# Two six-layer stacks on one core: the layer loops written out, and semaphore increments placed in front of some visits to small products on TensorE

## The chip, the cores and the metric

The kernel runs on one core of a Trainium2 chip. The metric is the device time of one launch in microseconds (us). Five engines work side by side, each through its own instruction stream: TensorE (PE; its weight loads are listed as PEld), VectorE (DVE), ScalarE (ACT), GpSimd (POOL) and SyncE (SP), which starts the DMA transfers. A "q" behind an engine's name (PEldq, SPq) marks what its sequencer does by itself: waits on semaphores, register work, branches and the start of transfers.

## The reference, cut to what matters

```python
x = L0_attn_a_X                                    # 8 x 256 x 128, f32
x = x + retention(layernorm(x))
x = x + ffn_stack(layernorm(x))                    # run 0
x = x + rwkv(layernorm(x))                         # mix and scan
x = x + ffn_stack(layernorm(x))                    # run 1

def ffn_stack(x):                                  # 6 layers, 2,048 rows of 128
    for i in range(6):
        x = attn_layer(shift_tokens(x), ...) + x   # 16 heads of 64, windows of 32 rows, each looking at 64 keys
        x = ffn_layer(shift_tokens(x), ...) + x    # layer norm, 128 -> 341 gated -> 128
    return x
```

The windowed attention is why there are small products: for each window of 32 queries and each head, a 32x64 block of scores, and then a 64x32 block of the weighed values. Everything is float32.

## The kernel before

The kernel has four parts: a retention layer, a stack (run 0), the mix-and-scan part, and a second stack (run 1). Both stacks come from `ffn_stack` and are the same code. The change touches the stacks alone.

**Tiling.** A stack works on tiles of 128 rows. There are 16 tiles in a layer and 96 (`TILES`) in a stack, 192 in all. Four tiles make a group (`GROUPS`), the unit of the feed-forward part. Work is cut into slots. In slot N each engine does pieces of several tiles, each with its lag: TensorE projects tile N-4, transposes tiles N-5 and N-6, computes the scores of tile N-6, weighs the values of tile N-9, projects out tile N-10, and does a quarter of the feed-forward part of an older group. The four kinds of slot (T = N mod 4, T0 to T3 in this text) are written out by hand in `slot`, one for each engine, and the order in them is fixed.

**TensorE's pieces.** `project` (L608) is a 128x512 product; `turn` (L617) four transpositions of 128x128; `project_out` (L668) eight accumulating 128x128 products; `center`, `variance`, `up` and `down` (L675, L682, L691, L701) the feed-forward part. `scores` (L632) is 64 products of 64x32 by 64x64, issued in two calls, and `weigh` (L655) is 64 products of 64x64 by 64x32, also in two calls. The text calls the 64 products of one tile a *visit*: there is one scores visit and one weigh visit for each tile. Each float32 product is two weight loads and two MATMULs in the stream of the chip, so a visit has 256 rows; a transposition has one of each.

**What sets the order.** Semaphores alone. [...] `apart` (L467) increments the semaphore `passed`, on which nobody waits; in front of a wait whose value is in a register it keeps waits in separate rows. For a slot whose number is a plain integer `apart` does nothing.

**The loops.** `slots` (L483 to L493) runs slots 0 to 15 written out, slots 16 to 79 as a hardware loop (`Fori`, L491) of two passes over 32 slots, and the last 32 written out. The four compute engines have this loop, and SyncE has one over layers 1 to 4 (L582). In the loops the slot's number is a register, so each wait value is worked out by register rows.

```python
            run_slots(0, 0, 0, 0, 16)
            with eng.Fori(0, 2) as pair:
                run_slots(32 * pair + 16, 8 * pair + 4, 2 * pair + 1, 1, 32)
            run_slots(16 * (DEPTH - 1), 4 * (DEPTH - 1), DEPTH - 1, 1, 16 + 16)
```

Of the kernel before, what the change touches and what calls it, by code (L numbers as in the profile page):

```python
# [20 lines left out]
DEPTH, HEADS, HD, WINDOW = 6, 16, 64, 32  # L21
# [318 lines left out]
RSQRT_SHIFT = 16  # L340
TABLE = "natural_log_exp_and_others"
GELU_TABLE = "gelu_and_others"


Group = namedtuple("Group", ("number", "layer", "row", "pair", "half"))
# [2 lines left out]
def ffn_stack(nc, shared, w):  # L348

    xo, ident, rot, mask = shared["x"], shared["ident"], shared["rot"], shared["mask"]  # L350
    with ExitStack() as ctx:
# [124 lines left out]
        def slots(eng, body):  # L476

            def run_slots(tile, group, layer, odd, slots_run):  # L480
                for n in range(slots_run):
                    def of(lag, k=n // 4):
                        return Group(group + (k - lag), layer + (k - lag) // 4, (k - lag) % 4, (k - lag) % 2,  # L483
                                     (odd + (k - lag) // 4) % 2)

                    def at(lag, n=n):
                        return tile + (n - lag), (n - lag) % 4, of(0, (n - lag) // 4)
                    body(tile + n, n % 4, group + n // 4, at, of)

            run_slots(0, 0, 0, 0, 16)  # L490
            with eng.Fori(0, 2) as pair:  # L491
                run_slots(32 * pair + 16, 8 * pair + 4, 2 * pair + 1, 1, 32)
            run_slots(16 * (DEPTH - 1), 4 * (DEPTH - 1), DEPTH - 1, 1, 16 + 16)  # L493

        block = ctx.enter_context(nc.Block())

# [1 line left out]
        def _(sp):  # L498
# [80 lines left out]
            load_mlp(0)  # L579
            sp.wait_ge(consts_set, N_CONSTS * (run + 1))  # L580
            layer_loads(0, True, False)
            with sp.Fori(1, DEPTH - 1) as layer:  # L582
                layer_loads(layer, False, False)
            layer_loads(DEPTH - 1, False, True)
            sp.wait_ge(wo_in, 16 * (layer0 + DEPTH))
# [13 lines left out]
        def _(pe):  # L599
# [11 lines left out]
            def turn(t, T, g, c):  # L611
                if not live(t):
                    return
                wait(pe, "united_" + c, t)
                bank = work[(BANK["t_" + c][T] + g.row) % 4]
                for n in range(4):
                    last = pe.transpose(bank[:, P * n:P * (n + 1)], roped[:, CHUNKS.index(c), T % 2, P * n:P * (n + 1)],  # L617
                                        ident[:, :])
                last.then_inc(done["turned_" + c], 1)

            def scores(t, T, g, part):
                if not live(t):
# [99 lines left out]
            def slot(N, T, G, at, of):  # L722
                if T == 0:
# [5 lines left out]
                    project(*at(4), "q0")  # L729
                    wait(pe, "kept_k0", N - 6)  # L730
                    up(of(4), "lin", 1)
                    wait(pe, "ot_set", N - 10)
                    weigh(*at(9), 0)
                    weigh(*at(9), 1)
# [5 lines left out]
                    project(*at(7), "v1")  # L740
                    wait_group(pe, "hid1", G - 4)
                    project(*at(4), "k1")
                    wait(pe, "masked0", N - 7)
                    wait(pe, "masked1", N - 7)
                    scores(*at(6), 0)
# [11 lines left out]
                elif T == 1:  # L757
                    wait(pe, "mid_set", N - 11)
                    project(*at(4), "k0")
                    wait(pe, "ot_set", N - 10)  # L760
                    weigh(*at(9), 0)
                    weigh(*at(9), 1)
# [16 lines left out]
                    project(*at(4), "k1")  # L779
                    wait(pe, "kept_k1", N - 6)  # L780
                    project(*at(4), "q1")
                    wait(pe, "masked0", N - 7)
                    wait(pe, "masked1", N - 7)
                    scores(*at(6), 0)
# [5 lines left out]
                elif T == 2:  # L790
# [5 lines left out]
                    center(of(3))  # L796
                    wait(pe, "kept_k0", N - 6)
                    down(of(4))
                    wait(pe, "ot_set", N - 10)
                    weigh(*at(9), 0)  # L800
                    weigh(*at(9), 1)
# [7 lines left out]
                    project(*at(4), "q1")  # L809
                    wait(pe, "kept_q0", N - 6)  # L810
                    project(*at(4), "k1")
                    wait(pe, "masked0", N - 7)
                    wait(pe, "masked1", N - 7)
                    scores(*at(6), 0)
# [17 lines left out]
                elif T == 3:  # L832
                    wait(pe, "v_out0", N - 6)
                    project(*at(4), "k0")
                    wait(pe, "ot_set", N - 10)
                    weigh(*at(9), 0)
                    weigh(*at(9), 1)
                    wait(pe, "kept_q0", N - 6)
                    project(*at(5), "v0")
                    wait(pe, "kept_k1", N - 6)  # L840
                    turn(*at(6), "q1")
                    wait(pe, "squared_q0", N - 4)
                    project(*at(7), "v1")
                    wait(pe, "squared_k0", N - 4)
                    project(*at(4), "k1")
                    wait(pe, "masked0", N - 7)
                    wait(pe, "masked1", N - 7)
                    scores(*at(6), 0)
                    scores(*at(6), 1)
                    wait(pe, "v_out0", N - 5)  # L850
                    up(of(3), "gate", 2)
                    wait(pe, "kept_q1", N - 6)
                    project(*at(4), "q1")
                    wait(pe, "v_out1", N - 7)
                    up(of(3), "gate", 0)
                    wait(pe, "squared_k1", N - 4)
                    project_out(*at(10))
                    wait_group(pe, "gelu2", G - 3)
                    turn(*at(5), "q0")
                    wait(pe, "squared_q1", N - 4)  # L860
                    up(of(3), "gate", 1)
                    wait_group(pe, "gelu0", G - 3)
                    turn(*at(5), "k0")
# [1745 lines left out]
```

## Time and profile before

| what | value |
|---|---|
| median of 3 runs | 3645.67 us (3636.82 to 3646.73) |
| the profiled execution: its own time | 3648.2 us |
| its span | 3646.4 us |
| mean granted TensorE clock | 0.967 of full speed |
| TensorE busy (MATMUL) | 3373.7 us, 93% |
| VectorE busy | 3341.6 us, 92% |
| GpSimd busy | 2706.3 us, 74% |
| ScalarE busy | 2049.2 us, 56% |

The span runs from the first to the last instruction of the profiled execution; its own time is 1.8 us more, for what lies around it. Shares of busy time are averages over the retention part, the two stacks and the part between them, which has its own limits. A MATMUL's end is modelled, so a small gap between two of them can be hidden in the busy time. A gap that is put down to "issue" is time in which the engine waited for nothing that the profile shows. The profile also lists each DMA queue. Queue q8 carries kind "instruction".

### The profile page before, as it was taken

How to read it: one execution, taken by the hardware profiler on the slowest of the kernel's cores; microseconds unless marked ns; L12 is line 12 of the kernel's file. 1: busy time of each engine (PE TensorE's matmuls, PEld its weight loads, DVE VectorE, ACT ScalarE, POOL GpSimd, SP SyncE). 2: the span in 40 equal slices, each digit the busy share in tenths (PEclk: the TensorE clock that was granted, in tenths of full speed). 3: DMA queues.
4: the chain of work that ended last, by engine and by line, in shares of the span. 5: the costliest groups of instructions: out<-in, count | busy, mean ns of one | idle time of the engine just before them, and what ended most of it. 6: DMA issues, size and time to landing. Idle time of an engine off the chain costs nothing. (4 is left out here: it accounts for less than half of the span.)

```text
span 3646.4 us, 153624 instructions
## 1 busy us (share of the span) xinstructions
PE 3373.7 (93%) x60144; PEld 2186.3 (60%) x60144; DVE 3341.6 (92%) x11899; ACT 2049.2 (56%) x3659; POOL 2706.3 (74%) x2440
## 2 busy tenths in 40 slices
PE   6799999999999999987699689999999999999997
PEld 4366666666666666652466446666666666666664
DVE  6899999999999999965799799999999999999995
ACT  2456666656665666644422155666666566666663
POOL 1788888888888888843144288888888888888882
PEclk9899999999999999998799699999999999999999
DMA  1233333333333333320000123333333333333332
GB/s 44 61 89 83 74 89 75 90 78 79 91 76 76 87 80 71 72 66 16 1 1 0 36 49 88 79 89 79 74 93 75 77 84 82 73 89 77 72 72 65
DMA packets 151851, 250.83 MB, mean 69 GB/s; under 512 B 42688, under 2 KB 73408, under 8 KB 150976
## 3 DMA queue, kind: packets, MB, share of 16 engines
q1 hardware_dynamic: 151104, 240.75, 27.7%
q8 instruction: 484, 7.93, 1.0%
q14 instruction: 263, 2.15, 0.2%
HBM read 38.21 MB, written 1.05 MB: 11 GB/s over the span
## 5 line engine op out<-in xcount | busy, mean ns | idle before, releaser
L608 PE MATMUL stack_work<-stack_w_qkv,stack_xst 128*128 128x512 f32 x2304 | 1173.6, 615 | 26.9 <-ACT stack_sq L881 16.7
L1337 POOL TENSOR_TENSOR stack_roped<-stack_rot_c,stack_rot_s 128x512 f32<-128x512 f32 x768 | 980.6, 1289 | 260.1 <-DVE stack_rot_s L1082 135.0
L1347 POOL TENSOR_TENSOR stack_roped<-stack_roped,stack_rnorm 128x512 f32<-128x512 f32 x768 | 791.5, 1044 | 162.4 <-DVE stack_rnorm L1114 162.4
L881 ACT ACTIVATE stack_sq<-stack_work 128x512 f32<-128x512 f32 x768 | 457.3, 595 | 735.0 <-DVE stack_rot_s L1082 727.5
L1080 DVE TENSOR_TENSOR stack_rot_c<-stack_work,rot_tables 128x512 f32<-128x512 f32 x768 | 517.0, 673 | 56.5 <-PE stack_work L608 52.0
L608 PEld LDWEIGHTS stack_work<-stack_w_qkv,stack_xst 128*128 128x128 f32 x2304 | 387.3, 193 | 300.5 <-issue 226.5
L1082 DVE TENSOR_TENSOR stack_rot_s<-stack_work,rot_tables 128x512 f32<-128x512 f32 x768 | 519.3, 676 | 1.1 <-issue 1.1
L1091 DVE TENSOR_REDUCE stack_ssq<-stack_sq 128x8 f32<-128x512 f32 x768 | 512.4, 672 | 3.3
L1125 DVE CUSTOM_DVE_ANT_0 stack_s_m<-stack_bank_s,band 128x64 f32<-128x64 f32 x3072 | 469.5, 215 | 30.1 <-PE stack_bank_s L632 26.4
L617 PEld LDWEIGHTS stack_work<-ident,stack_roped 128*128 128x128 f32 x3072 | 354.1, 141 | 167.4 <-issue 143.5
L617 PE MATMUL stack_work<-ident,stack_roped 128*128 128x128 f32 x3072 | 436.4, 277 | 19.3 <-ACT stack_sq L881 11.6
L1363 POOL TENSOR_TENSOR stack_s_m<-stack_s_m,stack_inv 128x512 f32<-128x512 f32 x384 | 412.6, 1074 | 37.8 <-DVE stack_inv L1143 37.8
L1355 POOL TENSOR_TENSOR stack_s_m<-stack_s_m,stack_smax 128x512 f32<-128x512 f32 x384 | 401.6, 1046 | 37.3 <-DVE stack_smax L1125 35.2
L655 PEld LDWEIGHTS stack_bank_o<-stack_p_pairs,stack_v_even 64*64 64x64 f32 x12288 | 330.0, 134 | 155.8 <-issue 155.6
L668 PEld LDWEIGHTS stack_work<-stack_o_t,stack_w_o 128*128 128x128 f32 x3072 | 364.5, 192 | 77.4 <-issue 63.8
L632 PEld LDWEIGHTS stack_bank_s<-stack_k_t,stack_q_t 64*32 64x32 f32 x24576 | 276.6, 105 | 206.2 <-issue 200.1
L655 PE MATMUL stack_bank_o<-stack_p_pairs,stack_v_nat 64*64 64x32 f32 x12288 | 378.2, 219 | 16.6 <-issue 16.5
L655 PE MATMUL stack_bank_o<-stack_p_pairs,stack_v_even 64*64 64x32 f32 x12288 | 378.8, 220 | 12.4 <-issue 8.8
L668 PE MATMUL stack_work<-stack_o_t,stack_w_o 128*128 128x128 f32 x3072 | 368.2, 275 | 5.2 <-issue 4.7
L632 PE MATMUL stack_bank_s<-stack_k_t,stack_q_t 64*32 64x64 f32 x24576 | 318.5, 225 | 48.0 <-issue 47.6
L655 PEld LDWEIGHTS stack_bank_o<-stack_p_pairs,stack_v_nat 64*64 64x64 f32 x12288 | 333.4, 135 | 20.2 <-issue 20.1
L907 ACT COPY stack_q_t<-stack_work 128x512 f32<-128x512 f32 x384 | 226.8, 591 | 169.0 <-PE stack_work L617 168.2
(255 smaller groups left out, 5093.2 us busy)
## 6 DMA issues: line engine op xcount, KB each, us to landing
stack_v_even<-stack_v_nat SPq DMA_DIRECT2D x768, 128.0 KB, 2.4
stack_p_pairs<-stack_p_turned SPq DMA_DIRECT2D x1536, 64.0 KB
stack_w_qkv<-table_ffn_qkv SPq DMA_DIRECT2D x192, 96.0 KB
stack_w_o<-table_ffn_wo SPq DMA_DIRECT2D x12, 512.0 KB, 3.9
stack_w<-table_ffn_w SPq DMA_DIRECT2D x12, 384.0 KB, 3.2
stack_w<-table_ffn_w SPq DMA_DIRECT2D x12, 192.0 KB, 3.0
x_outer<-L_attn_a_X SPq DMA_DIRECT2D x4, 256.0 KB, 8.1
ret_xpos<-table_xpos SPq DMA_DIRECT2D x1, 1024.0 KB, 7.5
```

The lines of the kernel that those rows point to most:

```text
L608: pe.matmul(work[(BANK["p_" + c][T] + g.row) % 4][:, :], xst[:, g.row, P * T:P * (T + 1)], w_qkv[:, g.half, col:col + 512], start=True, st ...
L617: last = pe.transpose(bank[:, P * n:P * (n + 1)], roped[:, CHUNKS.index(c), T % 2, P * n:P * (n + 1)], ident[:, :])
L632: last = pe.matmul(bank_s[j][WINDOW * n:WINDOW * (n + 1), 64 * hp:64 * hp + 64], q_t[rows, T % 2, hp, WINDOW * n:WINDOW * (n + 1)], k_t[ro ...
L655: last = pe.matmul(bank_o[HD * odd:HD * (odd + 1), two, at:at + WINDOW], values[:, 2 * m + j, :], p_pairs[rows, T % 2, odd_window, j, 2 * ...
L668: last = pe.matmul(bank[:, 0:P], w_o[:, g.half, n, :], o_t[:, T % 2, n, :], start=n == 0, stop=n == PAIRS - 1)
L881: act.activation(sq[:, i % 2, :], work[(BANK["p_" + c][T] + g.row) % 4][:, :], ACT.Square).then_inc(done["squared_" + c], 1)
L1080: dve.tensor_tensor(rot_c[:, i % 2, :].rearrange("p (h d) -> p h d", h=8), src.rearrange("p (h d) -> p h d", h=8), cosine, ALU.mult)
L1082: dve.tensor_tensor(rot_s[:, i % 2, :].rearrange("p (h f d) -> p h f d", h=8, f=2), src.rearrange("p (h f d) -> p h f d", h=8, f=2)[:, :, ...
L1091: dve.tensor_reduce(ssq[:, T % 2, i, :], sq[:, i % 2, :].rearrange("p (h d) -> p h d", h=8), AX.X, ALU.add).then_inc(done["summed_" + c], 1)
L1125: last = dve.tensor_tensor_reduce(s_m[:, T % 2, j, hp, :], bank_s[j][:, 64 * hp:64 * hp + 64], mask[:, first:first + 2 * WINDOW], 1.0, LOW ...
L1337: pool.tensor_tensor(roped[:, i, T % 2, :], rot_c[:, i % 2, :], rot_s[:, i % 2, :], ALU.add).then_inc(done["roped_" + c], 1)
L1347: pool.tensor_tensor(r, r, rnorm[:, T % 2, i, :].unsqueeze(2).broadcast_to([P, 8, HD]), ALU.mult).then_inc(done["united_" + c], 1)
```

## The change

It does three things.

1. `slots` no longer has a loop: all 112 slots of a stack are written out on the four compute engines, and SyncE's loop over layers 1 to 4 is a Python loop. All slot numbers are now integers, so the register rows, the branches and the increments of `apart` in the stacks are gone.
2. A table `SETTLE` gives, for each kind of visit, each run and each tile, a number of increments.
3. `settle` issues that many increments of `passed` on TensorE, each a semaphore row of its own, ahead of the waits that stand in front of the visit: before `wait(pe, "ot_set", N - 10)` for weigh, before `wait(pe, "masked0", N - 7)` for scores. Nothing waits on `passed`.

The order of all products, transfers and other work on every engine is as before.

```diff
+SETTLE = {
+    "scores": (
+        (0, 0, 0, 0, 0, 50, 0, 27, 0, 0, 0, 0, 0, 0, 0, 0, 0, 0, 0, 0, 0, 0, 0, 0,
...
+        (23, 59, 0, 126, 0, 0, 0, 0, 0, 0, 0, 0, 0, 0, 0, 0, 0, 0, 0, 0, 0, 0, 0, 0,
...
+    "weigh": (
+        (68, 0, 0, 0, 0, 0, 0, 0, 0, 37, 0, 27, 0, 43, 0, 27, 0, 43, 0, 27, 0, 43, 0, 27,
...
+         0, 43, 0, 27, 0, 43, 0, 27, 0, 43, 0, 27, 0, 43, 0, 27, 0, 43, 0, 36, 0, 0, 51, 0),
+        (0, 0, 0, 30, 0, 62, 0, 27, 0, 43, 0, 27, 0, 43, 0, 27, 0, 43, 0, 27, 0, 43, 0, 27,
...
+         0, 43, 0, 27, 0, 43, 0, 27, 0, 43, 0, 27, 0, 43, 0, 27, 0, 43, 0, 36, 0, 0, 51, 0),
...
-            run_slots(0, 0, 0, 0, 16)
-            with eng.Fori(0, 2) as pair:
-                run_slots(32 * pair + 16, 8 * pair + 4, 2 * pair + 1, 1, 32)
-            run_slots(16 * (DEPTH - 1), 4 * (DEPTH - 1), DEPTH - 1, 1, 16 + 16)
+            run_slots(0, 0, 0, 0, TILES + 16)
...
-            with sp.Fori(1, DEPTH - 1) as layer:
+            for layer in range(1, DEPTH - 1):
                 layer_loads(layer, False, False)
...
+            def settle(t, T, g, kind):
+                if live(t):
+                    for _ in range(SETTLE[kind][run][t]):
+                        pe.sem_inc(passed, 1)
...
                     up(of(4), "lin", 1)
+                    settle(*at(9), "weigh")
                     wait(pe, "ot_set", N - 10)
                     weigh(*at(9), 0)
                     weigh(*at(9), 1)
...
                     project(*at(4), "k1")
+                    settle(*at(6), "scores")
                     wait(pe, "masked0", N - 7)
                     wait(pe, "masked1", N - 7)
                     scores(*at(6), 0)
```

The two calls are added in the same way in all four kinds of slot. The table holds 3,526 increments. In its steady part, 41 times in a row over both runs, four tiles get 27 in front of one weigh visit (in a T0 slot, behind `up`) and 43 in front of another (in a T2 slot, behind `down`): 2,870 increments. The other 656 stand in front of 17 visits near the ends of the stacks, with 23 to 126 each.

## Rows read from the trace of the kernel before

**Rows 1.** The page: span, busy time, and 40 slices of PE and its clock.

```profile
span 3646.4 us, 153624 instructions
PE 3373.7 (93%) x60144; PEld 2186.3 (60%) x60144; DVE 3341.6 (92%) x11899; ACT 2049.2 (56%) x3659; POOL 2706.3 (74%) x2440
...
PE   6799999999999999987699689999999999999997
...
PEclk9899999999999999998799699999999999999999
```

**Rows 2.** Busy time in one stretch of the first stack: us, engines, PEclk, DMA.

```profile
600.00:1000.00 400.00, 386.83 (x7773) 253.09 (x7771) 382.03 (x1464) 247.43 (x445) 334.17 (x306) 0.99 0.34 81
```

**Rows 3.** PE's waits in that stretch: us in total, times, longest.

```profile
PE stack_bank_s L632 <- issue: 7.2, 6, 1.6
PE stack_work L608 <- DMA stack_w_qkv<-table_ffn_qkv: 3.0, 1, 3.0
PE stack_bank_o L655 <- issue: 1.9, 2, 1.4
```

**Rows 4.** The same view over the whole span.

```profile
PE stack_bank_s L632 <- issue: 47.6, 45, 2.0
PE stack_bank_o L655 <- issue: 25.2, 29, 1.9
```

**Rows 5.** PE in time order: a scores visit, then the end of a weigh visit.

```profile
996.58 1.52 PE L632 MATMUL stack_bank_s<-stack_k_t,stack_q_t 64*32 64x64 f32 x122
999.70 0.31 PE L632 MATMUL stack_bank_s<-stack_k_t,stack_q_t 64*32 64x64 f32 x6 [1.60 <-issue]
...
3321.16 0.32 PE L655 MATMUL stack_bank_o<-stack_p_pairs,stack_v_even 64*64 64x32 f32 x8
...
3324.25 0.26 PE L655 MATMUL stack_bank_o<-stack_p_pairs,stack_v_even 64*64 64x32 f32 x5 [1.26 <-issue]
```

**Rows 6.** DMA queues: over the span, then in 3321.5 to 3322.0 us.

```profile
q8 instruction: 484, 7.93, 1.0%
...
q8 instruction: 1, 0.02, 12.9%
```

**Rows 7.** The semaphore row in front of a weigh visit, at four visits.

```profile
L644 PEldq EVENT_SEMAPHORE  x1: 51/51/51, 3320.0 to 3320.0; - x1
L644 PEldq EVENT_SEMAPHORE  x1: 51/51/51, 1333.3 to 1333.3; - x1
L644 PEldq EVENT_SEMAPHORE  x1: 51/51/51, 1423.3 to 1423.3; - x1
L644 PEldq EVENT_SEMAPHORE  x1: 51/51/51, 3605.8 to 3605.8; - x1
```

**Rows 8.** Weight loads that open three of these visits, and one visit's gap.

```profile
1334.46 0.21 PEld L655 LDWEIGHTS stack_bank_o<-stack_p_pairs,stack_v_even 64*64 64x64 f32 x8 [0.76 <-issue]
...
1426.79 0.21 PEld L655 LDWEIGHTS stack_bank_o<-stack_p_pairs,stack_v_even 64*64 64x64 f32 x8 [0.76 <-issue]
...
3605.86 0.24 PEld L655 LDWEIGHTS stack_bank_o<-stack_p_pairs,stack_v_even 64*64 64x64 f32 x8 [1.67 <-issue]
...
3609.88 0.24 PE L655 MATMUL stack_bank_o<-stack_p_pairs,stack_v_nat 64*64 64x32 f32 x1 [1.93 <-issue]
```

**Rows 9.** PE's semaphore rows: apart's line (ns min/median/max), and two pairs that touch.

```profile
L467 PEldq EVENT_SEMAPHORE  x544: 51/51/1157, 270.7 to 3247.8; - x182
...
L449 PEldq EVENT_SEMAPHORE  x2: 51/51/51, 1275.2 to 1275.3; - x2
...
L449 PEldq EVENT_SEMAPHORE  x2: 51/51/51, 1320.8 to 1320.9; - x2
```

**Rows 10.** The loop's branch on PE and on DVE (ns min/median/max).

```profile
L491 PEldq COMPARE_BRANCH  x4: 83/1903/3767, 764.4 to 3255.5; - x4
...
L491 DVEq COMPARE_BRANCH  x4: 60/64/74, 766.0 to 3257.5; - x4
```

**Rows 11.** A stretch just behind a gap: the clock (0.50) in the third column from the end.

```profile
2226.30:2229.70 3.40, 3.40 (x9) 1.75 (x8) 2.10 (x8) 2.92 (x5) 3.21 (x3) 0.50 0.42 101
```

More of the change, by code:

```diff
@@ L342 @@
 GELU_TABLE = "gelu_and_others"
+SETTLE = {
+    "scores": (
[8 rows of a table added]
+    ),
+    "weigh": (
[8 rows of a table added]
+    ),
+}
 Group = namedtuple("Group", ("number", "layer", "row", "pair", "half"))
@@ L759, in slot @@
                     project(*at(4), "k0")
+                    settle(*at(9), "weigh")
                     wait(pe, "ot_set", N - 10)
@@ L781, in slot @@
                     project(*at(4), "q1")
+                    settle(*at(6), "scores")
                     wait(pe, "masked0", N - 7)
@@ L798, in slot @@
                     down(of(4))
+                    settle(*at(9), "weigh")
                     wait(pe, "ot_set", N - 10)
@@ L811, in slot @@
                     project(*at(4), "k1")
+                    settle(*at(6), "scores")
                     wait(pe, "masked0", N - 7)
@@ L834, in slot @@
                     project(*at(4), "k0")
+                    settle(*at(9), "weigh")
                     wait(pe, "ot_set", N - 10)
@@ L845, in slot @@
                     project(*at(4), "k1")
+                    settle(*at(6), "scores")
                     wait(pe, "masked0", N - 7)
```

10 rows, old and new, of the table SETTLE are left out of this document.

## The prediction

> **What bounds the kernel now.** I read the page first. TensorE is busy 93% of the span and VectorE 92%, and only the middle part between the stacks is loose [rows 1]. Then one stretch inside a stack: in 400 us TensorE computes for 386.8 us and VectorE for 382.0 us [rows 2]. TensorE bounds the stacks, with VectorE right behind. The 13.2 us in which TensorE did nothing have few causes: 9.1 us stand in front of scores and weigh products and are put down to "issue", which means that nothing in the profile held them, and 3.0 us are one late weight transfer [rows 3]. Over the whole span such gaps inside or at the visits come to 47.6 + 25.2 = 72.8 us in 74 places [rows 4].
>
> **What the gaps are.** In time order one can see one: 122 of 128 MATMULs of a scores visit run, then nothing for 1.60 us, then the last six. In the second example a weigh visit opens at 3321.16 and loses 1.26 us near its end [rows 5]. These products depend on nothing new. What does happen is a transfer of kind "instruction": queue q8 carries 484 of them with 7.93 MB, so 16.4 KB each, and 120,288 weight loads and MATMULs [rows 1] over 484 are 249 rows for each, which with the semaphore and register rows comes to about 256. One such transfer lies in 3321.5 to 3322.0, and products go on at 3324.25 [rows 5, 6]. So TensorE has run out of instructions. I counted the rows of the built program (four for a product, two for a transposition, one for any other) against all the gaps: within a stretch without a jump they all fall on one row modulo 256, and a gap appears only where that row is the 169th or a later one of a visit. A block that begins earlier in a visit never starves it. The request for the next block thus goes out when the sequencer is some 50 rows into a block, and what counts is the time from there to the block's end. In small products that time is short: a row takes 7.4 ns (252 rows from 3605.86 to the gap that ends at 3609.88, less 1.93 and the 0.2 us of the last MATMUL) [rows 8].
>
> **How late a block comes.** The sequencer passed the semaphore row in front of the second example at 3320.0 and the starved product started 4.25 us later. In another visit the row is at 3605.8 and the product at 3609.88, 4.1 us later [rows 5, 7, 8]. Where the request falls just behind that row, I take 3.3 to 4.2 us from the row to the block.
>
> **The change, part by part.**
>
> *Loops written out.* The loop's branch costs TensorE up to 3.77 us, in two of four cases [rows 10]: -7.5 us. On the other engines it is below 0.1 us. The register rows and the 544 increments of apart [rows 9] go away, but the sequencer runs over 1 us ahead of the products (1333.3 against 1334.46, 1423.3 against 1426.79 [rows 7, 8]), so they are hidden: 0, at most -5 us. If that lead were gone they would cost 0.1 us each.
>
> *The old gaps.* With the increments, four tiles have 2,560 rows, ten blocks, so the pattern locks. Counted on the built program, the starved row is then the 203rd of both padded weigh visits, the 171st and 175th of two scores visits, and at most the 88th of the other four. I leave 10 us for the scores visits and take the other 63 of the 72.8 us off. Bounds: -73 and -30 us.
>
> *The increments themselves.* The nearest rows are the semaphore rows of TensorE: each lasts 51 ns, but two that touch start 0.1 us apart [rows 9]. No row shows an increment without a wait, so the bounds are 0.051 and 0.11 us, and I take 0.1 us since it is what such a row costs the sequencer. In a T0 slot 27 of them take 2.7 us. The sequencer's lead there is 1334.46 - 1333.3 = 1.15 us [rows 7, 8], so the visit opens 2.7 + 0.1 - 1.15 = 1.65 us late. In a T2 slot 43 take 4.3 us against a lead of 3.5 us: 0.9 us late. Together 2.55 us in 41 steady periods: +105 us. The other 656 increments take 66 us, less some 2 us of lead at 17 visits: +32 us. At 0.051 us they come to about 15 and 5 us, at 0.11 us to 125 and 38. Queued behind an increment is all of TensorE's work, and what waits for the visit is ScalarE's copy and then `project_out`.
>
> *New gaps.* The increments stand in front of the row from which the next block is asked for, and they use up the lead. The visit then opens 0.1 us behind its semaphore row, as at 3605.8 and 3605.86 [rows 7, 8], and needs row 203 after 1.5 us. The block is there after 3.3 to 4.2 us: a gap of 1.7 to 2.6 us. The visit that opened with no lead lost 1.93 us with its starved row at 252 [rows 8]. If the request falls nine rows earlier, inside the increments, the block comes 0.9 us sooner. I take 1.4 us at 82 + 17 visits: +139 us. Bounds: 0 and 228 us.
>
> [...]
>
> *Sum.* -7.5 - 63 + 105 + 32 + 139 = +205 us of TensorE time. Little of it can hide: in 400 us only 13.2 - 9.1 = 4.1 us of TensorE's idle time is of another kind [rows 2, 3]. At worst 30% (4.1 of 13.2) is absorbed, at best none, and I take 15%: +175 us. The profiled execution took 3648.2 us, so 3823, and the median stands 2.5 us below it: **3820 us**.
>
> **Rivals.**
>
> *Cheap increments* (0.051 us each), with the new gaps: -7.5 - 63 + 15 + 5 + 139 = 88, times 0.85: 3720 us. For it: the row's own length. Against it: the touching pairs.
>
> *No gaps, dear increments.* The request goes out before the increments and the block lands while they run: -7.5 - 73 + 105 + 32 = 57, so 3695 us. For it: where the starved row comes before the 169th there is no gap. Against it: the counted position.
>
> *Faster.* Both at once: increments that cost about 0.05 us, hidden by the lead, and a block that is there in time. -7.5 - 73 + 15 + 5 = -60, times 0.85: 3595 us. It takes increments below about 0.07 us and no new gaps; above that the visit opens later than the gap it saves.
>
> *The clock falls.* [...] With two pauses at each padded visit this could come at many of the 99. Each costs up to 1.7 us of product time; at half of them 84 us more: 3900 us.
>
> *The table misses.* If the blocks lie otherwise than counted, the gaps stay as many as before and the increments are added: -7.5 + 105 + 32 = 130, so 3755 us.
>
> **How the numbers follow.** The forecast gets 0.47, cheap increments 0.12, no gaps 0.14, faster 0.12, the clock 0.10, the table 0.05. About 0.3%, 11 us, is what a measurement of this kernel can tell from no change. Only the case named faster lies below that, and a little of the second near it: faster 0.12, same 0.03, slower 0.85. The range reaches from just above no change to past the clock's case: 3655 to 3925 us, which leaves out the faster case and a tail above.
>
> **What would show it.** Right: TensorE's rows on the line of settle start 0.1 us apart; the idle time in front of the first weigh product of padded visits grows from 0.76 to over 2 us; issue gaps in weigh rise from 25 us to over 100 us and sit at the 203rd row; gaps in scores nearly vanish; about 493 transfers on q8. Wrong: increments 0.05 us apart, no gap behind the 203rd row, or VectorE's idle time swallowing the delays.

## The result, and the profile after

The changed kernel takes **4111.47 us** (median of 4, 4104.45 to 4116.39) against 3641.24 us (4 runs, 3634.68 to 3646.73) for the kernel before on the same chip: ratio 1.129, 95% interval [1.127, 1.131]. It is slower, as forecast, but by 470 us where 175 were forecast, and outside the range. All increments stand at line 643 now, scores is L656, weigh L679, `up` L715, `down` L725, `turn` L636, `project` L627.

The page of the changed kernel: span, busy time, slices of PE and its clock, and the instruction queue. They answer to [rows 1] and to the first of [rows 6].

```profile
span 4113.4 us, 154824 instructions
PE 3582.6 (87%) x60144; PEld 2387.5 (58%) x60144; DVE 3314.6 (81%) x11899; ACT 2050.4 (50%) x3659; POOL 2706.3 (66%) x2440
...
PE   6799999999999999988698678999999999999997
...
PEclk9899999999999999987898688999999999999998
...
q8 instruction: 492, 8.06, 0.8%
```

Two things are new. TensorE is busy for 209 us more than before (3582.6 against 3373.7) with the same 60,144 MATMULs: its mean granted clock fell from 0.967 to 0.893. And it stands idle more: 530.8 us of the span against 272.7. The waits of PE over the whole span say where, in the columns of [rows 4]:

```profile
PE stack_bank_o L679 <- issue: 311.6, 90, 8.9
PE stack_bank_s L656 <- issue: 36.7, 5, 18.2
```

Before, these two were 72.8 us in 74 places, nearly all inside visits. Now they are 348.3 us in 95 places, and 94 of them stand in front of a padded visit, that is, one with increments in front (the other, 0.8 us, opens an unpadded scores visit). Counted in the table, 95 visits are padded: 82 in the steady part and 13 near the ends of the stacks, not 17 as the section on the change says, nor 99 in all as the prediction took. Inside the visits nothing is left: two weight loads of a visit never start more than 0.20 us apart in any of the 384. PE in time order, the first products of a padded visit in a T2 slot and of one in a T0 slot, and the increments in front of each (sequencer rows; ns, first and last start in us):

```profile
957.81 0.44 PE L679 MATMUL stack_bank_o<-stack_p_pairs,stack_v_even 64*64 64x32 f32 x8 [3.25 <-issue]
923.01 0.44 PE L679 MATMUL stack_bank_o<-stack_p_pairs,stack_v_even 64*64 64x32 f32 x8 [3.21 <-issue]
```

```profile
L643 PEldq EVENT_SEMAPHORE  x43: 51/51/51, 951.0 to 957.6; - x43
L643 PEldq EVENT_SEMAPHORE  x27: 51/51/51, 918.6 to 922.8; - x27
```

43 increments take 6.6 us from the first to the last and 27 take 4.2 us: **0.157 and 0.162 us each**, not 0.1. (Nine in ten start 0.151 us apart, and about one in twenty 0.2 to 0.36.) The lead was about as predicted: 957.81 - 951.0 = 6.8 us, of which TensorE idled for 3.25, so 3.55 us (predicted 3.5), and 923.01 - 918.6 - 3.21 = 1.2 us (predicted 1.15).

What the clock does shows in stretches: the padded visit at 957.8 from its first to its last weight load, and for comparison the unpadded visit that opens at 938.95 (us; then PE and PEld busy; the granted clock is third from the end).

```profile
957.80:961.15 3.35, 3.34 (x126) 3.35 (x128) 0.50 0.44 106
938.95:940.80 1.85, 1.82 (x124) 1.82 (x127) 1.00 0.03 9
```

The same products take 3.35 us at 0.50 of the clock and 1.85 at 1.00. The clock fell before the pause was over. TensorE stopped at 954.56, 3.25 us ahead of 957.81, and the stretch up to the first product has a mean clock of 0.82:

```profile
954.00:957.80 3.80, 0.56 (x2) 0.02 (x1) 3.79 (x22) 1.09 (x2) 2.21 (x2) 0.82 0.08 21
```

So the last 1.4 us of it (0.18 of 3.8 us, times two) ran at 0.50, and the engine had stood for 1.9 us when the clock fell. Of the 192 weigh visits 85 take 3.3 us from the first to the last weight load, one takes 2.2, and all others at most 2.01. In [rows 2] the same 400 us had 386.8 us of PE and a clock of 0.99; now

```profile
600.00:1000.00 400.00, 362.28 (x6861) 247.37 (x6862) 333.83 (x1296) 219.31 (x392) 298.68 (x273) 0.91 0.29 70
```

Finally the block: in the increments of the visit at 957.8, 3.3 to 3.8 us ahead of its first product, one instruction transfer starts (DMA queues in 954.0 to 954.5).

```profile
q8 instruction: 1, 0.02, 11.9%
```

### The profile page after: what moved, and what is told of

It is laid out like the page before. It is cut to its first block and busy times, and to the rows that moved or that the text cites. A ratio compares the mean times of both kernels' runs of the same rounds, so it can differ in the third digit from the quotient of the medians.

```text
span 4113.4 us, 154824 instructions
## 1 busy us (share of the span) xinstructions
PE 3582.6 (87%) x60144; PEld 2387.5 (58%) x60144; DVE 3314.6 (81%) x11899; ACT 2050.4 (50%) x3659; POOL 2706.3 (66%) x2440
## 5 line engine op out<-in xcount | busy, mean ns | idle before, releaser
L627 PE MATMUL stack_work<-stack_w_qkv,stack_xst 128*128 128x512 f32 x2304 | 1203.7, 630 | 18.2 <-ACT stack_sq L913 14.5
L679 PE MATMUL stack_bank_o<-stack_p_pairs,stack_v_even 64*64 64x32 f32 x12288 | 500.7, 252 | 311.6 <-issue 311.6
L679 PEld LDWEIGHTS stack_bank_o<-stack_p_pairs,stack_v_even 64*64 64x64 f32 x12288 | 437.1, 173 | 459.0 <-issue 459.0
L627 PEld LDWEIGHTS stack_work<-stack_w_qkv,stack_xst 128*128 128x128 f32 x2304 | 406.9, 203 | 295.8 <-issue 222.5
L636 PE MATMUL stack_work<-ident,stack_roped 128*128 128x128 f32 x3072 | 491.5, 302 | 16.4 <-ACT stack_sq L913 10.8
L636 PEld LDWEIGHTS stack_work<-ident,stack_roped 128*128 128x128 f32 x3072 | 402.0, 156 | 176.6 <-issue 157.0
L679 PE MATMUL stack_bank_o<-stack_p_pairs,stack_v_nat 64*64 64x32 f32 x12288 | 499.5, 251 | 0.0
L679 PEld LDWEIGHTS stack_bank_o<-stack_p_pairs,stack_v_nat 64*64 64x64 f32 x12288 | 441.9, 174 | 0.0
L1395 POOL TENSOR_TENSOR stack_s_m<-stack_s_m,stack_inv 128x512 f32<-128x512 f32 x384 | 401.6, 1046 | 45.1 <-DVE stack_inv L1175 45.0
L939 ACT COPY stack_k_t<-stack_work 128x512 f32<-128x512 f32 x384 | 225.2, 604 | 334.8 <-PE stack_work L636 334.3
L656 PEld LDWEIGHTS stack_bank_s<-stack_k_t,stack_q_t 64*32 64x32 f32 x24576 | 277.2, 106 | 187.8 <-issue 182.4
```

Source lines behind the costliest of these rows:

```text
L627: pe.matmul(work[(BANK["p_" + c][T] + g.row) % 4][:, :], xst[:, g.row, P * T:P * (T + 1)], w_qkv[:, g.half, col:col + 512], start=True, st ...
L679: last = pe.matmul(bank_o[HD * odd:HD * (odd + 1), two, at:at + WINDOW], values[:, 2 * m + j, :], p_pairs[rows, T % 2, odd_window, j, 2 * ...
L939: act.copy(out, src).then_inc(done["kept_" + c], 1)
```

## The experiments

My theory after the result: the increments are the whole loss, by their own time of 0.155 us each where the lead ends, and then by the half clock behind each pause; the blocks arrive while they run. The rivals: the written-out program costs; rows cost wherever they stand; the alignment starves TensorE; the clock costs little. All kernels below are edits of the changed kernel. The row positions, counted on each built program, are the changed kernel's where nothing else is said.

### Loops written out alone, and the same increments elsewhere

`e1_unrolled`:

```diff
...
             def settle(t, T, g, kind):
-                if live(t):
-                    for _ in range(SETTLE[kind][run][t]):
-                        pe.sem_inc(passed, 1)
+                return
...
```

> Loops written out, no increment at all. My theory (the 3,526 increments are the whole loss: about 0.155 us each of TensorE's time, then a clock at half speed during the visit behind each pause): the loss is gone and only the two late branches are saved, so 3615 to 3650 us, granted clock 0.96 to 0.97, gaps inside visits of 60 to 100 us as before. Rival (the written-out program itself costs, by more instruction blocks or a worse place of the starved row): above 3700 us, with the extra time as gaps inside visits.

Measured: 3605.99 us, ratio 0.991 [0.990, 0.993]; clock 0.968. Page and PE's waits (scores L654, weigh L677):

```profile
span 3609.9 us, 151302 instructions
PE 3368.3 (93%) x60144; PEld 2184.6 (61%) x60144; DVE 3352.4 (93%) x11899; ACT 2046.3 (57%) x3659; POOL 2704.2 (75%) x2440
...
PE stack_bank_s L654 <- issue: 35.4, 31, 2.0
PE stack_bank_o L677 <- issue: 11.5, 16, 1.5
```

The written-out program is faster than before, by 32 us (the ratio is against 3635.86 us, the kernel before in runs beside it; each ratio below is taken in the same way), and TensorE's busy time is that of before. It came 9 us below my range, with smaller gaps than I expected: the gaps in and at visits are 46.9 us in 47 places, 26 less than before. The increments alone cost 4111 - 3606 = 505 us. In the trace's own rows of TensorE, taken in order, the 44 gaps that lie inside a visit all start on one row modulo 256, to within a row, in both stacks. TensorE's rows in this trace, 122,650 with those of its sequencer, over the 479 transfers of q8 make 256.1 for each (123,144 over 484 in before, with its jumps: 254.4; 126,172 over 492 after the change: 256.4). So the gaps do go with blocks of 256 rows.

`e2_spread`: from tile 11 to 89 the increments of weigh visits are divided among the wide products ahead of the visit, in four shares in a T0 slot (shown) and in six in a T2 slot.

```diff
...
                 if T == 0:
+                    share(*at(9), 0)
                     wait(pe, "mid_set", N - 11)
                     project(*at(4), "k0")
+                    share(*at(9), 1)
                     wait(pe, "kept_q0", N - 6)
                     up(of(4), "lin", 0)
+                    share(*at(9), 2)
                     wait_group(pe, "gelu1", G - 4)
                     project(*at(4), "q0")
+                    share(*at(9), 3)
                     wait(pe, "kept_k0", N - 6)
                     up(of(4), "lin", 1)
...
```

> The same number of increments before the same row of the program, but for tiles 11 to 89 split into shares of 6 to 8 in front of the wide products of the slot (4 shares in a T0 slot, 6 in a T2 slot). My theory: each share takes 0.9 to 1.2 us of the sequencer while a 128x512 product keeps TensorE busy, so the pause in front of the padded visits falls from 4.2 to about 1 us and the clock stays near 0.96; 3600 to 3720 us. New gaps of 0.3 to 1.9 us at the 203rd row of the padded visits may show, since the block has no longer 4 us in which to come. Rival (rows cost wherever they stand, since the sequencer is the bound): 3950 us or more, with the pauses now in front of the wide products.

Measured: 3768.91 us, ratio 1.036 [1.035, 1.038]; clock 0.957. PE's waits (weigh L686, scores L663, `up` L722, `down` L733):

```profile
PE stack_bank_o L686 <- issue: 55.1, 10, 9.0
PE stack_bank_s L663 <- issue: 38.0, 6, 17.9
...
PE stack_work L722 <- issue: 18.2, 71, 1.4
...
PE stack_work L733 <- issue: 17.1, 80, 0.3
```

The 93 us in 16 places are the increments near the ends, which were not spread. The rest of what the kernel lies above e1_unrolled (163 us) is 70 us for the 2,800 increments that were spread, which in one piece make up some 505 - 93 = 412 us (both net of the gaps that the alignment saves). So rows do not cost the same wherever they stand, but a share of 7 is not wholly hidden either (0.2 to 0.3 us in each of 151 places, as the last two lines show), and the time came 49 us above my range.

`e4_behind` (the same in all four kinds of slot):

```diff
...
-                    settle(*at(9), "weigh")
                     wait(pe, "ot_set", N - 10)
                     weigh(*at(9), 0)
                     weigh(*at(9), 1)
+                    settle(*at(9), "weigh")
...
```

> The increments of weigh visits stand behind the visit instead of in front, so the visit runs with its starved row at 230 or 246 and the pause comes after it. My theory: the same pauses, about 340 us, now in front of a turn or a projection, and gaps of 0.6 to 1.9 us back inside the padded visits; the clock falls as before but over the wide products behind; 4080 to 4220 us. Rival (what costs is only the delay of the visit, and behind it the increments hide under waits that are there anyway): below 3900 us.

Measured: 4264.53 us, ratio 1.172 [1.171, 1.174], worse than the change by about 155 us; clock 0.893. PE's waits (`turn` L636):

```profile
PE stack_work L636 <- issue: 460.5, 87, 11.5
...
PE stack_bank_o L679 <- issue: 34.0, 39, 1.9
```

The pauses are now in front of `turn` and longer, 5.3 us each instead of 3.5, since behind a row of small products the sequencer has hardly any lead (the last weight load of the visit starts 0.12 us after the first increment in T0 slots and 0.18 in T2 slots, medians); and 39 gaps at weigh visits are back. Of the 40 steady T0 visits 32 have one, at about the 230th row; the 40 steady T2 visits, with the starved row at the 246th, have none. The time came 45 us above my range, by that lead, which I had left out.

### The rows kept, the increments replaced by products

`e3_products` and `e6_same` (the second with the products on the visit's four quarters in turn):

```diff
+            def parts(kind, t):
+                n = SETTLE[kind][run][t]
+                return (n % 4, n // 4)
...
-                    for _ in range(SETTLE[kind][run][t]):
+                    for _ in range(parts(kind, t)[0]):
                         pe.sem_inc(passed, 1)
...
+                    for _ in range(parts("weigh", t)[1]):
+                        pe.matmul(bank_o[0:HD, 0, 0:WINDOW], v_even[0:64, T % 2, 0, :, :][:, 0, :],
+                                  p_pairs[0:64, T % 2, 0, 0, 0, :], start=True, stop=True)
                 for gp in range(2):
...
```

> Rows at the same places, but of each number n of increments only n mod 4 remain (3 for 27 and for 43), and the others become n div 4 float32 products of four rows each (a first product of the visit, written to a place that the visit writes again). My theory: a row costs 7 ns instead of 155, the pause is gone, the clock is back at 0.96, and the starved row lies at 203 as after the change; since nothing gives the block time, the new gaps that I predicted (0.5 to 2 us) come at part of the 99 visits: 3590 to 3700 us. Rival (the alignment itself lowers the clock or starves TensorE): above 3800 us.

> As e5_shift without the 35 rows: the padded visits keep the 203rd row. My theory: 20 to 30 us faster than e3_products by the cheaper products, and slower than e5_shift by the gaps at the 203rd row alone, 30 to 90 us: 3620 to 3655 us. Rival (position without effect): equal to e5_shift.

Measured: 3673.67 us, 1.010 [1.007, 1.012], and 3666.04 us, 1.006 [1.003, 1.009]; clocks 0.969 and 0.961. With as many rows at the same places, the loss of 470 us is down to 20 to 40. So it hung on what the rows are, not on where they put the block. But here the gap at the 203rd row does come. PE's waits of e3_products (weigh L689), one such gap in time order, and the queue in 962.0 to 962.1, as that visit opens:

```profile
PE stack_bank_o L689 <- issue: 26.1, 41, 1.2
```

```profile
963.53 0.31 PE L689 MATMUL stack_bank_o<-stack_p_pairs,stack_v_even 64*64 64x32 f32 x3
964.20 0.24 PE L689 MATMUL stack_bank_o<-stack_p_pairs,stack_v_even 64*64 64x32 f32 x2 [0.36 <-issue]
```

```profile
q8 instruction: 1, 0.02, 60.0%
```

Where no increments give it time, the transfer runs while the visit already does, and the visit starves at its 203rd row. In tiles 11 to 89 that is 36 of 40 T0 visits and none of 40 T2 visits, though both have the starved row at the 203rd: the T2 visit has 3.5 us of lead and the T0 visit 1.2. How far behind a block a visit starves is thus not one row number, as I had read it; it goes with the lead in front. e8_half, below, bears that out: where 23 increments use up the lead of the T2 visits, 17 of 40 starve.

e6_same missed its range by 11 us, and it is not told apart from e3_products (the intervals overlap; I expected 20 to 30 us less). Its products are cheaper, 0.03 us each against 0.1, some 49 us in all, but its visits then open earlier and starve for longer: 34 of 40 T0 visits with 1.16 us each, against 0.64 us in e3_products. Its waits in weigh (L694):

```profile
PE stack_bank_o L694 <- issue: 49.6, 42, 1.9
```

`e5_shift` and `e9_shift17` are e6_same with everything moved earlier by 35 or 17 rows, once; `e10_lead` is e9_shift17 with 7 and 19 increments among the 27 and 43 rows. The edit of e5_shift (e9_shift17 has `("weigh", 0, 0): 17`):

```diff
+SHIFT = {("weigh", 0, 11): 35}
...
+            def parts(kind, t):
+                n = SETTLE[kind][run][t]
+                n += SHIFT.get((kind, run, t), 0)
+                return (n % 4, n // 4)
...
```

> As e3_products (n mod 4 increments, the rest as products of four rows), with two edits: the added products go round the visit's own quarters of TensorE, so that each should cost 29 ns instead of 61, and one visit of the first stack gets 35 rows more, once, so that from there on every starved row lies 35 rows earlier: at the 168th or before in all eight visits of four tiles. My theory: where the starved row is before the 169th there is no gap, so both the new gaps of e3_products and the old ones of e1_unrolled (65 us) are gone and only 0.3 to 0.5 us of added products for four tiles is paid: 3550 to 3590 us, faster than all others. Rival (gaps are no matter of position but of whatever stands in front): 3640 us or more with gaps as in e3_products.

> As e5_shift, but 17 rows more instead of 35, at the first padded visit of the kernel: the starved row then lies at the 186th in the padded weigh visits, at the 158th and 154th in two scores visits, and no longer right behind a scores visit, where e5_shift had 33 gaps of up to 1.2 us. My theory: weigh visits were never starved at 177 to 190 in before's steady part, so the 18 us behind the scores visits go and nothing comes back: 3570 to 3595 us. Rival (186 is too late, gaps of 0.5 to 1 us at the padded weigh visits): 3615 us or more.

> As e9_shift17, but as many increments as the sequencer's lead should hide: 7 of 27 rows and 19 of 43, the other rows products (5 and 6). My theory: 7 increments take 1.1 us against 1 us of lead, 19 take 2.9 us against 3.4 us, so they cost nothing and 5 products of 29 ns are saved for four tiles: 0 to 10 us faster than e9_shift17. Rival (part of each increment shows even under a lead): 10 to 40 us slower than e9_shift17.

Measured: e5_shift 3605.66 us, 0.990 [0.986, 0.993]; e9_shift17 3628.32 us, 0.996 [0.995, 0.998]; e10_lead 3625.3 us, 0.994 [0.993, 0.996]. The padded visits of e5_shift, with the starved row at the 168th, have no gap in the steady part, but the last rows of a scores visit and the `turn` behind it starve instead:

```profile
PE stack_bank_s L668 <- issue: 11.2, 21, 1.7
PE stack_work L637 <- issue: 8.5, 16, 1.3
```

So e5_shift missed its range by 16 us. e9_shift17 mends that and has gaps at about the 186th row of T0 visits, 15 of 40. It missed its range by 33 us, and its rival held: neither shift was without a loss somewhere. The added products, 10 and 6 for four tiles, cost some 20 us besides: they delay a T2 visit by 0.31 and a T0 visit by 0.20 us, 41 times. e5_shift is level with e1_unrolled and no better; these two are the fastest kernels of this study, both 1% faster than before. e10_lead is not told apart from e9_shift17 (3 us, and the intervals overlap): increments inside the lead cost nothing that shows.

### The price of a row

`e7_waits`:

```diff
                     for _ in range(SETTLE[kind][run][t]):
-                        pe.sem_inc(passed, 1)
+                        pe.wait_ge(consts_set, N_CONSTS)
+                        pe.wait_ge(consts_set, N_CONSTS)
```

> Each increment is replaced by a row with two waits that have long been met; as many rows, at the same places. In the trace of before, two such rows touch at 0.1 us, which is the price that I had put on an increment. My theory (the price of the row decides, 0.155 us for an increment and 0.105 us for a met wait): the 3,526 rows cost 3,526 times 0.05 = 176 us less, and the half clock stays at most padded visits: 3900 to 3960 us. If the shorter pause no longer brings the half clock, some 60 to 130 us less again: 3780 to 3870 us. Rival (any semaphore row that is issued in a long run costs 0.155 us): 4100 us as after the change.

Measured: 3793.9 us, ratio 1.041 [1.038, 1.044]; clock 0.944. PE's waits (weigh L680, scores L657), and the 25 rows in front of the T0 visit near 929 us:

```profile
PE stack_bank_o L680 <- issue: 159.1, 90, 5.8
PE stack_bank_s L657 <- issue: 24.7, 5, 12.5
```

```profile
L643 PEldq EVENT_SEMAPHORE  x12: 51/51/51, 926.6 to 929.1; - x12
L644 PEldq EVENT_SEMAPHORE  x13: 51/51/51, 926.4 to 929.2; - x13
```

25 rows in 2.8 us and a little more than 0.1 us for each (median 0.106 us over the kernel): the price that the prediction had, from the touching pairs of [rows 9], is right for rows that only wait. The rival, 0.155 us for any row in a long run, is refuted. The time is over 100 us below my range of 3900 to 3960, and in the one that I gave for no half clock at all, though part of the half clock is still there. That 3794 us is near the first forecast of 3820 is luck: this kernel has none of the new gaps of that sum, 139 us, and has a cost of the clock that the sum had not. The pauses shrink by 348.3 - 183.8 = 164.5 us (3,526 times 0.05 is 176). Weigh visits that take over 2.3 us fall from 85 to 35. Of the 40 T2 visits in tiles 11 to 89, whose pause is now 1.3 us, none is slowed; of the 40 T0 visits, with 2.0 us, 36 run in part at half clock.

`e8_half`, from e6_same:

```diff
-                return (n % 4, n // 4)
+                p = n // 8
+                return (n - 4 * p, p)
```

> Rows at the same places, 15 and 23 of 27 and 43 rows are increments and the rest products. My theory: 15 increments are 2.3 us against 1 us of lead, 23 are 3.6 us against 3.4 us, so the pauses fall from 3.25 us each to 1.4 and 0.2 us; the half clock comes at few or none of the visits; 3680 to 3780 us. Rival (a pause of any length in front of a visit brings the half clock): 3850 us or more, with visits of 3.3 us instead of 1.8.

Measured: 3732.11 us, ratio 1.024 [1.020, 1.027]; clock 0.961. In the middle of its range. PE's waits (in front of the visits L684 and L659, inside them L667 for scores and L695 for weigh):

```profile
PE stack_bank_o L684 <- issue: 82.4, 78, 5.0
PE stack_bank_s L667 <- issue: 31.3, 37, 1.7
PE stack_bank_s L659 <- issue: 16.2, 4, 8.7
PE stack_bank_o L695 <- issue: 11.5, 30, 1.4
```

With 15 and 23 increments the pauses are 98.6 us instead of 348.3, and the clock is nearly that of e1_unrolled. Gaps inside visits are back, 42.8 us: the block no longer has the whole time of 27 or 43 increments. In tiles 11 to 89 the pauses are 1.35 us in T0 slots and 0.2 us in T2 slots, and none of these 80 visits runs at a lower clock: a pause of that length does not bring the half clock here.

### The pause and the clock

`e11_lump` and `e12_broken`: 19 and 35 increments and two products, in this order, or with a third of the increments behind each product. From e11_lump to e12_broken:

```diff
-                    for _ in range(rest):
+                    for _ in range(rest - 2 * (rest // 3)):
                         pe.sem_inc(passed, 1)
                     for k in range(few):
...
+                        for _ in range(rest // 3):
+                            pe.sem_inc(passed, 1)
```

> Rows at the same places as after the change. In front of a weigh visit all but 8 rows are increments in one piece (19 of 27, 35 of 43), then two small products. My theory of the pause: 19 x 0.155 - 1 = 1.9 us and 35 x 0.155 - 3.4 = 2.0 us instead of 3.25 us, on top of the usual 0.8 us; with pauses near 2.8 us the clock falls at some of the padded visits, as in e7_waits: 3830 to 3930 us. If it falls at all of them: 3950 to 4000 us.

> The same increments and the same two products as e11_lump, but a third of the increments behind each product, so that no piece of idle time is over about 2 us while the idle time in all is the same. If the clock falls because of one long pause, the padded visits keep the full clock and the kernel is 40 to 120 us faster than e11_lump. Rival (it falls because TensorE does little in all, whether in one piece or in three): within 20 us of e11_lump, with the same number of visits at half clock.

Measured: 3890.74 us, 1.068 [1.065, 1.071], and 3882.34 us, 1.064 [1.061, 1.067]; clocks 0.942 and 0.935. The idle time of e12_broken is in two kinds of place (L688 the added products, L701 weigh):

```profile
PE stack_bank_o L701 <- issue: 100.1, 92, 2.9
PE stack_bank_o L688 <- issue: 68.4, 86, 3.1
```

That makes 1.1 and 0.8 us on average, and the clock is no higher for it. The idle time is not the same, as I had wanted it, but less: in tiles 11 to 89 it is 1.4 us at a T0 visit and 1.8 at a T2 visit, in pieces of at most 0.8 and 1.4 us, against 1.9 and 2.4 us in one piece in e11_lump. Yet 51 weigh visits run in part at half clock, against 37 in e11_lump. So breaking a pause with two small products does not keep the clock up, and the rival holds in the main: the times are 8 us apart, though the number of slowed visits is not the same.

`e13_busy` keeps the delay and fills it with work:

```diff
+                    for _ in range(3):
+                        pe.matmul(bank_o[:, 0, :], ident[:, :], w_qkv[:, near.half, 0:512], start=True, stop=True)
```

> As after the change, with the same number of rows before each visit, but in the 27 and 43 rows of the steady part the time is filled with work: 3 increments, three added 128x512 products (12 rows, their result is written over by the visit) and 3 or 7 small ones. Everywhere else the increments stay. Three wide products are 2.6 to 3.0 us, nearly the 3.25 us by which the increments delay a visit. My theory (a pause costs its own length and then, by the half clock behind it, 1.5 us in the visit and about 1 us in the products that follow): the delay stays and the half clock goes from some 80 visits, so 3850 to 3930 us, about 200 us less than after the change. Rival (the clock costs only the 1.5 us in the visit): 3960 to 4010 us. Second rival (VectorE, which waits for the delayed visits, sets the time, and the clock costs nothing): 4050 us or more.

Measured: 3851.3 us, ratio 1.060 [1.058, 1.062]; clock 0.960. PE's waits (weigh L696, scores L666), then 400 us of the first stack in this kernel and in the changed one:

```profile
PE stack_bank_o L696 <- issue: 49.4, 9, 8.8
PE stack_bank_s L666 <- issue: 38.1, 6, 18.0
```

```profile
1000.00:1400.00 400.00, 400.00 (x7561) 258.27 (x7560) 365.52 (x1417) 241.27 (x431) 324.10 (x296) 1.00 0.33 80
```

```profile
1000.00:1400.00 400.00, 364.63 (x6862) 247.90 (x6862) 331.66 (x1286) 216.06 (x389) 290.63 (x266) 0.91 0.31 74
```

The steady pauses are gone (what is left are 15 near the ends of the stacks) and the clock is 1.00. The six added wide MATMULs (three products) start 0.43 us apart and take 2.6 us. From the start of the last MATMUL in front to the visit's own first, a padded visit now takes 3.19 us in T0 and 3.31 us in T2 slots, against 3.80 and 3.83 after the change and 0.52 in e1_unrolled. So a visit is only 0.6 or 0.5 us less late than after the change, some 46 us in all. Yet the kernel is 0.070 of before's time, 254 us, faster, at the lower edge of my range and far below both rivals. The other **208 us or so are the half clock**. TensorE's busy time says the same: 3582.6 - 3368.3 = 214 us more after the change than in e1_unrolled, for the same MATMULs.

The clocks alone give an estimate of the same cost. In the changed kernel wide MATMULs start 0.85 us apart at 0.50 (L627 at 962.29 us) and 0.43 at 1.00 (964.50 us), so I take half of the time at half clock as lost. Mean clocks of 0.893 and 0.960 are 880 and 308 us at half clock, and half of the difference is 286 us. The runs show 208 to 214. A part of each such stretch lies on the pause itself, where no product is slowed: counting only the time at half clock in which TensorE is busy, 664 us after the change and 180 us in e13_busy, half of the difference is 242 us. The rest is not accounted for.

## Why the prediction was wrong, step by step

The direction was right; the forecast change, 175 us, was too small by 295. Two steps failed for most of it: the price of an increment, and the clock, which the sum put at nothing. A third, the new gaps, failed the other way and hid part of the miss. Measured, from the kernel before: 3641, less 32 for the loops, less the 47 us of gaps that e1_unrolled has left, plus 348 of pauses, plus 214 of clock, is 4124; the change takes 4111.

- **The branch and the loops, -7.5 us.** Measured -32 us [-38, -26] in e1_unrolled. Some 26 of them are gaps inside visits that the written-out program happens not to have (72.8 to 46.9 us), since its blocks fall elsewhere; the other 6 are about what the two late branches took.
- **The old gaps, -63 us.** Right in effect: no visit has one now.
- **The price of an increment, 0.1 us (bounds 0.051 and 0.11).** This is the step that failed first. The nearest row was a pair of waits, and a row that increments costs 0.157 us in a run; e7_waits shows both prices side by side. The leads taken against it were right to 0.1 us. The terms "+105" and "+32" were thus 137 us for what measured 348 (and the 32 counted 17 visits where the table pads 13). At 0.155 us the same working gives 27 x 0.155 + 0.1 - 1.15 = 3.1 and 43 x 0.155 - 3.5 = 3.2 us, and 41 x 6.3 = 258 us for the steady part; the profile has 348.3 - 87.5 = 261. So the term's form was right and its price was not, and the upper bound should have stood well above the dearest row of another kind.
- **The new gaps, +139 us.** They did not come: 0 us. "No gap behind the 203rd row" was among the prediction's own signs of being wrong. It saw that a request inside the increments brings the block sooner, and took 0.9 us off; in fact the increments behind the start of the transfer last 3.0 to 3.6 us at T2 visits and 1.6 to 2.8 us at 33 of the 41 steady T0 visits, and the block was there before the visit ran out. The prediction's some 50 rows from the start of a block to the request are not what the transfers show: they start 20 to 24 increments ahead of the visit at all 41 that have 43, and 11 to 19 ahead at those 33 of the 41 weigh visits that have 27, so 28 to 41 rows into the block; at the other 8 they start before the first increment. On this its second rival, "no gaps, dear increments", was right, with a time of 3695 us that lacked the same price and the clock. With products in place of increments the gaps do come, at T0 visits: 26 us in e3_products and 50 us in e6_same, where the 1.2 us at each is near the 1.4 us of the prediction. Even then the term would have been three to five times too large, since T2 visits do not starve; and it multiplied by 99 visits where 95 are padded.
- **The clock, a rival at 0.10 worth 84 us.** It came at 85 weigh visits and cost 214 us. The main sum had no term for it, though [rows 11] showed the half clock, 3.4 us at 0.50, behind a pause of 1.6 us that ends at 2225.2 us in a weigh visit. The rival was priced on the visit alone (up to 1.7 us, half of the 3.4 us of [rows 11]), and the products behind it ran at half clock too: 85 x 1.49 = 127 us in the visits, which leaves some 87 behind them. And it stood as a case of its own, with the short pauses of the forecast. A dearer increment lengthens the pause, so price and clock go up together; the range treated them as separate mishaps.
- **15% absorbed.** Measured next to nothing: the terms add to 4124 us without it, 13 us more than the kernel took, 2% of pauses and clock together.
- **What would show it.** Rows 0.1 us apart: wrong, 0.151 to 0.157. Idle time in front from 0.76 to over 2 us: right, 3.2. Issue gaps in weigh over 100 us: right, 311.6, but in front of the visits and not at the 203rd row, which named the wrong cause. Gaps in scores nearly vanish, and 492 transfers: right.

Some of the prediction's figures do not follow from its own working, without weight for the result: at 0.051 us an increment the steady part comes to 13 us and the rest to nothing (15 and 5 there), at 0.11 us the steady part to 129 (125 there), the row of small products to 7.5 ns (7.4 there), and the upper end of the new gaps, 2.6 us at 99 visits, to 257 us (228 there).

What stays open: why an increment costs 0.05 us more than a met wait, why a pause of 2.0 us slows most T0 visits of e7_waits and not all, and the some 30 us between 242 and what the clock cost.

## What to carry to other kernels

A filler row is priced by a row of its own kind or bounded far above the nearest other; in front of a T0 visit the same 27 rows take the sequencer 4.2 us as increments and 2.8 as met waits, while as six small products and three increments they delay the visit by 0.2. A pause of some 3 us on TensorE was paid twice here, once by its length and again by the half clock around and behind it, so a term for such a pause needs the second price in the same sum, and filling it with work that nobody needs made the faster of the two kernels. Before aligning a stream by hand, write the loops out and measure that alone: here it was all the gain there was, and the best alignment found added nothing to it.

## What the runs showed of the hardware

- An increment row on TensorE is listed with 51 ns but follows the one before at 151 ns (157 on average); a row of met waits follows at 106 ns (113 on average, e7_waits).
- At half clock the small products of a weigh visit take 3.31 instead of 1.82 us, 1.8 times as long.
- In tiles 11 to 89, pauses of 3.2 us in front of a visit slowed 78 of 80 visits, pauses of 2.0 us 36 of 40 in part, and pauses of 1.3 to 1.4 us none of 80 (after the change; T0 of e7_waits; T2 of e7_waits and T0 of e8_half). In e12_broken pieces of at most 0.8 us with two small products between them slowed 21 of 40 T0 visits in part.
- A visit with its starved row at the 203rd is starved with 1.2 us of lead in front and not with 3.5 us. In e1_unrolled 479 instruction transfers go with 47 gaps at the small products, 46.9 us together.
- In 400 us of e13_busy TensorE is busy for 400.00 us at a clock of 1.00, with the semaphores of four other engines in between. In that stretch no wait on another engine shows as a gap of TensorE; the ends of its MATMULs are modelled, so small ones can be hidden, and the added products may cover others.
- In the trace of before TensorE's sequencer has 2,440 semaphore rows, 406 register rows and 4 branches, and SyncE's has the 2,564 starts of transfers. The 64 products of a visit are 128 weight loads and 128 MATMULs (24,576 of each in 192 visits).
- In the loops of before the two waits for data in front of a weigh visit stand in two rows of `apart` (L467, at 1005.92 and 1006.17 us, each with one wait and the increment); in the slots written out they share one row of L644 (at 1333.3 us).
